# A transformer layer on one core: experts 0 and 1 visited by sets of images, products with V side by side, tokens stationary for the gate, weight splits on GpSimd

## What is computed

```python
x = x + attention(ln_c(x))            # 8 heads of 64, q, k, v and output projections 512 x 512, with biases
t = tokens(x)                         # (8, 1024, 512)
n2 = ln_t(t)
affinity = softmax(n2 @ gate_weight)  # 16 experts, (8, 16, 1024)
gating, index = top_k(affinity, 128)  # each expert takes 128 tokens of each image
h = gelu(n2[index] @ w1[e] + b1[e])
t[index] += gating * (h @ w2[e] + b2[e])
```

## Time and profile before

| what | value |
|---|---|
| time, median of 3 runs | 3197.95 us (3191.12 to 3199.35) |
| profiled execution, its own time | 3197.93 us |
| its span, first to last instruction | 3196.1 us |
| mean granted clock of TensorE | 0.987 |
| PE busy | 3062.6 us (96%) |
| PEld, DVE busy | 2629.6 us (82%), 2291.5 us (72%) |
| ACT, POOL busy | 1850.8 us (58%), 1093.3 us (34%) |

### The profile page before, as it was taken

One profiled execution on the slowest core, in us unless ns is written; L12 is line 12 of the kernel. 1 busy time (PEld: TensorE's weight loads), 2 busy tenths in 40 slices (PEclk: granted clock), 3 DMA queues, 4 the chain that ended last, 5 costly groups with the idle time before them and its releaser, 6 DMA issues. The chain is left out here.

```text
span 3196.1 us, 49855 instructions
## 1 busy us (share of the span) xinstructions
PE 3062.6 (96%) x18116; PEld 2629.6 (82%) x18116; DVE 2291.5 (72%) x3580; ACT 1850.8 (58%) x3353; POOL 1093.3 (34%) x1113
## 2 busy tenths in 40 slices
PE   6999999999999999999999999999938999999998
PEld 5988889888878888888888888889826888888886
DVE  5878688678768876886888788678764655655653
ACT  3876678477747756783876578478712333333332
POOL 1225123412513251342225123412513444444443
PEclk9999999999999999999999999999978999999999
DMA  7122221321231232113213221311134566566564
GB/s 237 37 60 106 65 60 51 116 68 37 71 122 37 64 116 64 54 57 106 68 43 107 84 60 44 113 51 37 41 116 109 123 147 142 121 145 143 122 145 59
DMA packets 121614, 283.60 MB, mean 89 GB/s; under 512 B 22464, under 2 KB 30656, under 8 KB 110656
## 3 DMA queue, kind: packets, MB, share of 16 engines
q1 hardware_dynamic: 92736, 213.72, 20.2%
q0 software_dynamic: 28672, 67.13, 11.9%
HBM read 173.08 MB, written 74.15 MB: 77 GB/s over the span
## 5 line engine op out<-in xcount | busy, mean ns | idle before, releaser
L802 DVE TENSOR_TENSOR PT<-ring,PT 128x512 fp32r<-128x512 f32 x1024 | 676.5, 686 | 161.0 <-ACT PT L535 142.6
L535 ACT ACTIVATE PT<-ring 128x512 fp32r<-128x512 f32 x1024 | 582.9, 598 | 170.7 <-PE ring L929 87.5
L961 PE MATMUL O<-PT,V 128*128 128x256 f32 x4096 | 673.3, 289 | 0.0
L734 DVE TENSOR_REDUCE nmax<-S 128x1 f32<-128x1024 f32 x512 | 619.7, 1211 | 54.2 <-PE S L918 54.1
L929 PE MATMUL ring<-ident,prob 128*128 128x128 f32 x4096 | 614.1, 273 | 16.3 <-DVE PT L802 12.9
L961 PEld LDWEIGHTS O<-PT,V 128*128 128x128 f32 x4096 | 575.5, 189 | 40.3
L918 PE MATMUL S<-kd,qs 128*128 128x512 f32 x2048 | 599.1, 414 | 2.1 <-ACT prob L526 1.7
L526 ACT ACTIVATE prob<-S,nmax 128x1024 f32<-128x1024 f32 x512 | 571.1, 1115 | 36.0 <-DVE nmax L734 36.0
L464 POOL COPY oS<-oHL 64x256 f32<-64x256 f32 x256 | 100.8, 394 | 1283.6 <-ACT oHL L584 1278.1
L929 PEld LDWEIGHTS ring<-ident,prob 128*128 128x128 f32 x4096 | 464.3, 139 | 55.7 <-issue 48.9
L918 PEld LDWEIGHTS S<-kd,qs 128*128 128x128 f32 x2048 | 347.1, 189 | 50.4 <-issue 5.3
(11 more groups left out here) (132 smaller groups left out, 3461.5 us busy)
## 6 DMA issues: line engine op xcount, KB each, us to landing
kd<-kd SPq DMA_DIRECT2D x128, 256.0 KB, 3.7
wraw<-w_dram SPq DMA_DIRECT2D x32, 1024.0 KB, 7.0
wqk<-wqk_split SPq DMA_DIRECT2D x24, 1024.0 KB, 4.8
xt<-x_dram SPq DMA_DIRECT2D x16, 1024.0 KB, 7.8
Rs<-rinv_rows SPq DMA_DIRECT2D x56, 256.0 KB, 3.4
PT<-wv_split SPq DMA_DIRECT2D x7, 2048.0 KB, 8.8
oT<-x_dram SPq DMA_DIRECT2D x24, 512.0 KB, 3.3
out_dram<-oT SPq DMA_DIRECT2D x48, 256.0 KB, 8.2
```

What stands on the lines that cost most here:

```text
L535: nc.scalar.activation(PT[:, 0, u // 2 % 2, 4 * c:4 * c + 4, u % 2 * P:u % 2 * P + P], ring[:, k % 2, :].rearrange("p (m q) -> p m q", m=4 ...
L734: nc.vector.tensor_reduce(nmax[:, s:s + 1], S[:, s % 2, :], AX.X, ALU.max, negate=True).then_inc(max_done, 1)
L802: nc.vector.tensor_tensor(PT[:, 1, here[0], here[1], here[2]], ring[:, k % 2, :].rearrange("p (m q) -> p m q", m=4), PT[:, 0, here[0], her ...
L961: last_mm = nc.tensor.matmul(O[:, m % 2, 0:QC], V[:, t, head // 2, 2 * (head % 2):2 * (head % 2) + 2, :].rearrange("p h d -> p (h d)"), PT ...
```

## The change

It has five parts.

- *Unit*: in `turn_and_multiply` both quarters of products with V come first, then both halves of the transposes.
- *Gate*: the tokens are the stationary side and the gate's 16 columns move, so the logits come out with tokens on the partitions; `copy_logits` and the transposes of L1085 are gone. The softmax starts from these logits ahead of the maximum of unit 1. The affinities' transposes move between the two halves of unit 1 of the next image, their copies behind that unit's copies.
- *Prologue*: GpSimd makes the low parts of V's and k's weights, VectorE those of q and of the output projection. Stores start as each matrix is split, and ScalarE's first copies wait for the stores of their own staging tiles alone.
- *Early visits*: the first four visits are (expert 0, images 0-3), (expert 1, images 0-3), (expert 0, images 4-7), (expert 1, images 4-7), written out. The picks for images 4 to 7 are interleaved with VectorE's work for the first two visits; there ScalarE makes the high parts of h and of the weights and GpSimd the low parts. Later visits keep their order.
- *Loads*: w1, w2 and the biases have semaphores of their own; the weights of an expert are loaded as soon as the split before has freed `wraw`.

```diff
@@ prologue: stores, first copies, GpSimd's splits
+            for j in range(2):
+                sp.wait_ge(w_lo[1 + j], 1)
+                for h in range(2):
+                    store_split(0, j, h, w0_out)
...
+            sp.wait_ge(w0_out, 16 * 4)
+            load_first_pair()
+            for j, h, n in ((0, 0, 0), (0, 1, 0), (1, 0, 1), (1, 1, 2)):
+                for p in range(1, PAIRS):
+                    store_split(p, j, h, w_out[n])
...
+            for w in (0, 2):
+                pool.wait_ge(w_hi, w + 1)
+                raw, hi, lo, _ = splits[w]
+                nc.gpsimd.tensor_tensor(lo, raw, hi.bitcast(F32), ALU.subtract).then_inc(w_lo[w], 1)
...
-            act.wait_ge(w_out, 16 * 4 * (PAIRS - 1))
-            high_of_proj(0, 0)
+            act.wait_ge(w_out[0], 16 * 2 * (PAIRS - 1))
+            high_of_proj(0, 0, 0, 2)
+            act.wait_ge(w_out[1], 16 * (PAIRS - 1))
+            high_of_proj(0, 0, 2, 4)
@@ unit (TensorE)
+                    if m >= 0:
+                        for c in range(2):
+                            product_with_v(m, 2 * half + c)
                     for c in range(2):
-                        if m >= 0:
-                            product_with_v(m, 2 * half + c)
                         turn_probs(b, u, c)
+                        if u == 1 and c == 0 and b > 0:
+                            turn_affinities(b - 1)
@@ gate (TensorE), softmax (VectorE), copies (ScalarE)
-                    last_mm = products(O[0:E, i // 4, i % 4 * P:i % 4 * P + P],
-                                       [(gate_sb[:, c, :], n2T[:, i % 2, c, :]) for c in range(KC)])
+                    last_mm = products(O[:, 0, i * E:(i + 1) * E],
+                                       [(n2T[:, i % 2, c, :], gate_sb[:, c, :]) for c in range(KC)])
...
-                dve.wait_ge(logits_turned, b + 1)
+                dve.wait_ge(logits, b + 1)
...
+                if not last:
+                    maximum(b + 1, 1)
                 dve.wait_ge(soft_exp, b + 1)
...
                     high_of_probs(b, s - 2)
+                    if s == 3 and b > 0:
+                        copy_affinities(b - 1)
@@ experts: SyncE
-                    sp.wait_ge(ws_lo, (e + k) * WCH + 2 * WCH)
+                    sp.wait_ge(ws_lo, (e + k) * WCH + 2 * WCH - KC)
                     sp.sem_inc(sp_passed2, 1)
+                    load_w1(e + k + 2)
+                    load_w2(e + k + 2)
                     sp.wait_ge(y0_done, (e + k) * (2 * G) + 2 * G)
-                    load(e + k + 2, k)
+                    load_biases(e + k + 2, k)
@@ experts: GpSimd, early visits
+            pool.wait_ge(chosen, 2)
+            early_gather(0)
+            low_of_weights(0, KC)
+            early_gather(1)
+            low_of_h(0)
+            low_of_weights(1, 0)
+            early_scatter(0)
+            low_of_h(1)
             pool.wait_ge(chosen, 4)
+            early_gather(2)
+            early_scatter(1)
+            early_gather(3)
@@ experts: ScalarE, visit 0
+            for m in range(KC):
+                gelu(0, 0, m)
+                high_of_h(0, m)
+            high_of_weights(1, 0)
+            high_of_weights(1, 1)
+            for j in range(2):
+                turn(1, 1, j)
+                high_of_weights(1, 2 + j)
@@ experts: VectorE, early visits
+            for j in range(G):
+                turn(0, 0, j)
+                pick(j, j + 1)
+            dve.wait_ge(b12_in[0], 32)
+            pick(G, 18)
+            turn(1, 1, 0)
+            turn(1, 1, 1)
+            pick(18, 21)
+            for j in range(G):
+                if j in (1, 2):
+                    turn(1, 1, 1 + j)
+                add_b2(0, 0, j)
+                pick(21 + j, 22 + j)
+            pick(25, PICKS)
...
+            add_b2(1, 1, 0)
             join_halves(1)
+            for j in range(1, G):
+                add_b2(1, 1, j)
...
+                    add_b2(v, v % 2, j)
+                    if v == 3:
+                        split_chunk(2, 0, KC + j)
```

More of the change, by code:

```diff
@@ L641, in image @@
                     high_of_probs(b + 1, 0)
-                for i in range(2):
-                    act.wait_ge(affT_filled, b * 2 + i + 1)
-                    nc.scalar.activation(affT[:, 512 * i:512 * i + 512], O[0:E, 1 - i, :], ACT.Copy
-                                         ).then_inc(affT_copied, 1)
+                if last:
+                    copy_affinities(b)
             all_images(act, image)
@@ L931, in turn_probs, with turn_affinities @@
                 last_t.then_inc(ring_filled, 1)
+            def turn_affinities(j):
+                pe.wait_ge(soft, j * 5 + 5)
+                for h in range(2):
+                    for i in range(4):
+                        last_t = nc.tensor.transpose(O[0:E, 1 - h, i * P:(i + 1) * P], aff[:, 4 * h + i, :], ident)
+                    last_t.then_inc(affT_filled, 1)
             for i in range(NT):
@@ L1091, in image @@
                     scores(b + 1, 2)
-                pe.wait_ge(soft, b * 5 + 5)
-                for h in range(2):
-                    for i in range(4):
-                        last_t = nc.tensor.transpose(O[0:E, 1 - h, i * P:(i + 1) * P], aff[:, 4 * h + i, :], ident)
-                    last_t.then_inc(affT_filled, 1)
+                if last:
+                    turn_affinities(b)
             all_images(pe, image)
@@ L1196, in experts, with later_experts @@
         WCH = 2 * KC
-        def every_expert(engine, expert):
-            expert(0, 0, False)
-            expert(1, 1, False)
-            with engine.Fori(1, E // 2 - 1) as twos:
+        def later_experts(engine, expert):
+            expert(2, 0, False)
+            expert(3, 1, False)
+            with engine.Fori(2, E // 2 - 1) as twos:
                 expert(2 * twos, 0, False)
@@ new lines, in scatter, with early_column, early_gather @@
+            def scatter(x, j, image, column):
+                pool.indirect_dma_start(
+                    out=out_rows, out_offset=bass.IndirectOffsetOnAxis(ap=column, axis=0),
+                    in_=y[:, x, j, :], in_offset=None, compute_op=ALU.add,
+                ).then_inc(added[image], 16)
+            def early_column(v, j):
+                at = v % 2 * B + G * (v // 2) + j
+                return idx[:, at:at + 1]
+            def early_gather(v):
+                if v >= 2:
+                    pool.wait_ge(xr_filled, (v - 1) * G)
+                for j in range(G):
+                    gather(v % 2, j, early_column(v, j))
@@ new lines, in early_scatter, with later_gather, later_scatter @@
+            def early_scatter(v):
+                for j in range(G):
+                    image = G * (v // 2) + j
+                    pool.wait_ge(y_done, v * G + j + 1)
+                    if v % 2:
+                        pool.wait_ge(added[image], 16)
+                    scatter(v % 2, j, image, early_column(v, j))
+            def later_gather(e, k, g):
+                for j in range(G):
+                    gather(g, j, idxc[:, k, G * g + j:G * g + j + 1])
+            def later_scatter(e, k, g):
+                for j in range(G):
+                    image = G * g + j
@@ L1417, in join_halves, with pick @@
                                         ).then_inc(chosen, 1)
+            def pick(n0, n1):
+                if n0 == 0:
+                    dve.wait_ge(aff_in, 32)
+                for n in range(n0, n1):
+                    pick_step(nc, dve, n, work[:, :], best_b, pos_b, picked_b)
             reverse_second_half(0, best_a, pos_a)
@@ L1486, in _ @@
+            turn_choice(0)
+            pe.wait_ge(rows_made, 1)
             for j in range(G):
                 turn(0, 0, 0, j)
-            every_expert(pe, expert)
+            pe.wait_ge(first_w1_lo, KC)
+            project_1(0, 0, 0)
+            turn(0, 1, 1, 0)
+            turn(0, 1, 1, 1)
+            pe.wait_ge(ws_lo, split_chunks(0))
+            for j in range(G):
+                if j in (1, 2):
+                    turn(0, 1, 1, 1 + j)
+                project_2(0, 0, j)
+            pe.wait_ge(ws_lo, split_chunks(0) + KC)
@@ new lines, in _ @@
+            project_1(1, 1, 1)
+            pe.wait_ge(ws_lo, split_chunks(1))
+            for j in range(G):
+                if j == 2:
+                    turn_choice(1)
+                project_2(1, 1, j)
+            pe.wait_ge(rows_made, 2)
+            for j in range(G):
+                turn(1, 2, 0, j)
+            for v in (2, 3):
+                k = v % 2
+                project_1(v, k, k)
+                for j in range(2):
+                    turn((v + 1) // 2, v + 1, 1 - k, j)
+                for j in range(G):
+                    if j in (1, 2):
+                        turn((v + 1) // 2, v + 1, 1 - k, 1 + j)
+                    project_2(v, k, j)
@@ L1491 @@
+            later_experts(pe, expert)
 _OUT = "out_dram"
```

350 lines of the change are left out of this document (213 added, 137 removed).

## The result

The changed kernel takes 3165.7 us, the median of 8 runs (3155.5 to 3183.5); the kernel before took 3196.8, the median of 8 runs made beside them. The ratio is 0.9906, with a 95% interval from 0.9886 to 0.9925: 30 us less by the ratio, 31 between the medians, where 26.5 were forecast. The sum came out well by luck, since errors of both signs met in it.

A forecast was written before the change was run, and what follows sets the result against it. TensorE was taken as 90% busy or more nearly everywhere, with a hole where experts begin. Terms -4 + 3 + 2.5 - 1 + 0 - 24 + 2 - 5 = -26.5 took 3198 to 3171.5 us; range 3148 to 3189.

The forecast's parts named there:

- Units: -4 forecast: Attention units: products with V side by side save 0.01 us in each of 440 units, -4 us (-40 to +22).
- the sum of 2.71: New attention unit in us: scores 1.00, two times 0.46 for products, 0.85 less 0.06 for eight transposes; before 2.72.
- Rival A: Attention unit: side-by-side order really saves its switches, -40 instead of -4, ending at 3135 us; chance 0.07.
- B: Rival: ScalarE's chain exceeds 2.71, TensorE waits in all 440 units, 3211 us; chance 0.05. In times, the experts' stage start.
- Gate and step: +5.5 forecast: Gate tiles +3 us (eight matmuls 0.92 against 0.87, 64 tiles); step between images +2.5 us (scores 5 later, 7 steps).
- rival D: Gate matmuls as cheap as the 0.57 row (-25 instead of +3), prologue -6: 3138 to 3150 us; chance 0.10.
- Image 7: -1 forecast: Last image, no next one: experts' stage begins earlier by the logits' transposes of 0.57 and one copy, -1 us.
- Prologue: 0 forecast: Start: earlier store release offset by GpSimd's V split delaying normalisation; ScalarE ready near 58.5 as now, 0 us (-6 to +3).
- Experts: -24 to visit 2 forecast: Experts' stage: early visits overlap the picks; visit 2 at 83.3 instead of 107.3 after stage start, -24 us (-30 to -16).
- Rival C: Experts' early visits: overlap doesn't happen, visit 1 stands still until picks end; gain down to 8, 3188 us; chance 0.12.
- Visit 4: +2 forecast: Before visit 4 TensorE waits for the last weight split, now behind visit 3's last sum, +2 us.
- Later visits: -5 forecast: TensorE's waits for VectorE's turn go, as loads come earlier and w1 is waited for alone: 12 x 0.45, -5 us.

The follow-up runs named there:

- wide gate: Changed kernel with 64 moving columns instead of 16 in every matmul of the gate (its 16 columns four times over): 3152.8 us, ratio 0.9863.
- alternated unit: Changed kernel with the old order inside a unit put back (quarter of the products, half of the transposes, quarter, half): the run took 3167.9 us.
- broken gate: Changed kernel, 16 columns, with the last 12 matmuls of the next image's projections moved from ahead of the gate to behind its third tile: 3201.3 us, ratio 1.0012.
- held w1: Changed kernel with 64 moving gate columns, and the load of expert 1's w1 held until the four first gathers have landed: 3154.2 us (1 run).
- attention by itself: Changed unit order, gate and prologue, with the experts' stage of the kernel before: 3188.5 us, ratio 0.9974.

## Why the prediction was right, point by point

The total was within 6 us, in the forecast's own range. That is luck in part: with the clock held by the wide gate the same kernel takes 3152.8, 19 us below the forecast. The terms were not all right: against -4, +5.5, -1, 0, -24, +2 and -5 stand +2, -13.5 at full clock with +11 of low clock on top in the profiled run, +3.7, -3.2, -24.0, +2.4 and -7.5. These make -29; the spans differ by 30.5. (The +2 is against the alternated unit in the changed kernel.)

**Units: -4 forecast, +2 measured.** The step that failed is the sum of 2.71. Its transposes were right (0.85 - 0.06 = 0.79, measured 0.79). The eight products were taken as twice 0.46 and took 0.95, the scores 1.01 instead of 1.00: 2.74 to 2.75. A gain of 0.01 per unit was within the grain of the records, whose rows of the same thing differ by up to 0.03. Rival A falls with it, and B does not come: ScalarE's 0.66 became waits of 0.29 and 0.57 for the ring, and TensorE waits in none of these units.

**Gate and step: +5.5 forecast, -13.5 measured at full clock** (from the eight transposes ahead of the gate to scores 5 it takes 23.69 instead of 25.62, seven times). Two steps failed. The eight matmuls were put at 0.92, the row of the products, against 0.87 for those they replace; they took 0.81, and the row itself has 0.97 for the old ones (no row shown has 0.87): -0.16 instead of +0.05. And the forecast priced only these eight, though the tile has a second part: from the transposes to the next matmuls it takes 0.47 instead of 0.59. A tile is 0.28 shorter, over 64 tiles -18. The softmax was to come 0.3 to 0.4 later at scores 5; from scores 0 to scores 5 it takes 12.47 instead of 12.70, though TensorE waits for scores 3 and 5 (0.64 and 0.58) as feared. So rival D (-25) was nearer on the gate than the forecast's +3, though not by its row of 0.57, and the time did not show it, because the clock fell. The Trainium skill, TensorE: Matmul & The Clock Gate, section LDWEIGHTS, gives columns divided by 1.2, 107 ns for 128 whatever the rows; the eight take 101 ns each here and 105 with 64 columns moving, so it was nearer than the row that the forecast chose.

**The clock among the gate's tiles: not in the forecast.** It read 1.00 in a stretch of attention where TensorE is busy nearly all the time, and had no term for the clock between images. TensorE was busy there too, and lost it: in 8 of 21 steps of the three traces with 16 moving columns, in none of 49 with 64. That the moving side does it is shown by that one edit, which leaves loads, order and waits alone. The Trainium skill, in the same page, HAM oscillation — how this bites in real kernels, ties the fall to idle gaps between bursts of matmuls; the traces here show a fall without a gap, and one behind a gap of 1.3 us (the broken gate). Why it strikes some steps and not others is open.

**Image 7: -1 forecast, +3.7 measured.** The step has no term for the clock behind the wait for VectorE. B came 1.2 to 2 us earlier in the three kernels where the clock was back after 7 us (52.6 instead of 53.9), and 3.5 to 5 later where it stayed low, as in the profiled run.

**Prologue: 0 forecast, -3.2 measured.** The Newton step and the k split went as forecast, 4.23 each. What failed is the step "ScalarE is ready near 58.5": V's chain ended 0.6 us later instead of 2. The forecast left out that ScalarE's wait for the q and k weights, ahead of all tokens before (20.62), now stands behind the first two copies; with VectorE's splits these come at 17.69, and the chain 3 us earlier. GpSimd's splits spent that gain again. And TensorE, which before ran at half clock from 60.7 to some 64, now kept 1.00; by the first exponential the gain is 1.4 larger (no run takes the two apart). The Trainium skill, SBUF — State Buffer, section SBUF: two separate sides, has the engine that comes second at the shared port wait for the other's whole instruction: 0.17 without GpSimd's split, 4.23 with it, agrees. The Trainium skill's warning in that section, that GpSimd can't write descriptors, speaks of VectorE's two-port modes; the forecast stretched it to weight splits, which are subtractions with two inputs, and priced +2.8. It came to little: the first gather's four issues took 0.95 to 1.19 us, the longest beside those splits but one of 1.17 ahead of them, and visit 1's took 0.94 to 0.97.

**Experts: -24 to visit 2 forecast, -24.0 measured.** The steps cancel here too. The tokens were to be there at B + 12 and came at B + 15.3, beside the load of w1 for expert 1, issued with the fourth gather; with that load held back they came at B + 12.7. Projection 0 so came 2.9 later; its 48 matmuls took 12.8 instead of 13.6; the 5.1 us of waiting ahead of the nineteenth pick are the 6 of the forecast; the picks ended at B + 65.6 instead of 64.2. VectorE's chain set visit 2, as the forecast had it: with its idle time taken out and GpSimd's and TensorE's order to match, visit 2 moves by 7 us beyond what the held w1 gives, to B + 73. Rival C did not come: the overlap happened.

**Visit 4: +2 forecast.** It starts 25.86 us behind visit 3, not 23.65: 2.2 (the table's +2.4 has two other visits in it). **Later visits: -5 forecast, -7.5 measured.** The wait was rightly placed, its cause was half named: w1 being waited for alone does it, the earlier loads would have done only part. The forecast left 0.18 per visit for VectorE's own splits; TensorE's line shows no such wait at all.

## What to carry to other kernels

A stretch is fast only as long as its neighbours let it be: measure a thinner instruction by a row of its own, and then look at the granted clock over a whole run of them; here a wider moving side, at 0.03 us for eight matmuls, held it. Where two transfers or a chain are tied by one wait, split the wait first: it cost nothing and gave the whole gain here. And find whose chain sets the end of a stage, and move its work into the idle time ahead of it: fourteen picks moved, with the order around them, were worth 7 us, the order of 440 units 2.

## What the hardware showed that was not expected

The granted clock fell to 0.50 while TensorE's records lie end to end (6.00 of 6.00 us busy, then 12.00 of 12.00 at 0.50), on tiles of eight matmuls with 16 moving columns and four transposes, and in none of 49 steps with 64 columns at the same tile time (1.28 and 1.29 us). In the changed kernel and in the attention by itself a fall lasted 10.2 or 13.7 us and cost 4.8 to 7.2. Four times the moving columns cost 0.03 us for eight matmuls. Eight matmuls that load 128 columns and move 16 took 0.57 us where the load has 16 rows (the transposes of logits) and 0.81 where it has 128.
